# Turning x and the normalised residual by DMA, and moving the output projection, in a cross-attention and FFN kernel

## The reference, cut to what matters

```python
x = x + xattn(layernorm(x), ctx)      # 4 batches, 512 rows, 512 columns
x = x + ffn(layernorm(x))             # 1376 inner columns

def xattn(x, y):                      # 16 heads of 32
    q = ln(x @ Wq + bq)               # normalised per head
    k, v = ln(y_main @ Wk + bk), y_main @ Wv + bv        # the 496 first context rows
    k2, v2 = ln(y_dca @ Wkv_dca + ...), ...              # the 16 last ones
    return (softmax(q k) v + softmax(q k2) v2) @ Wo + bo

def ffn(x):                           # weights are lut[idx], 16 entries
    return (silu(x @ gate) * (x @ up)) @ down
```

## Time and profile before

| | |
|---|---|
| median of 3 runs | 907.59 us (905.56 to 909.68) |
| profiled execution | 908.92 us |
| its span | 907.1 us |
| PE / DVE / ACT / POOL busy | 88% / 58% / 54% / 27% |
| mean granted TensorE clock | 0.964 of full speed |

### The profile page before, as it was taken

How to read it: one execution, slowest core, us unless ns; L and a number is a source line. 1 busy time by engine, 2 the same in 40 slices (tenths; PEclk the granted TensorE clock), 3 DMA queues, 4 the chain that set the end, 5 groups by cost and what they waited for, 6 DMA issues and landing times.

```text
span 907.1 us, 15618 instructions
## 1 busy us (share of the span) xinstructions
PE 799.5 (88%) x5892; PEld 319.0 (35%) x5892; DVE 522.1 (58%) x934; ACT 487.4 (54%) x964; POOL 240.8 (27%) x284
## 2 busy tenths in 40 slices
PE   3756666699889999999899999999999999979998
PEld 1321122233345333332444333334443332234443
DVE  7759999687564888221646984216458940052220
ACT  3456567677335788554246886652558865511100
POOL 7693100000156222100472222003732210002320
PEclk9986688899999999999999999999999999999999
DMA  8349844354400000112000000101000000000001
GB/s 266 98 135 293 222 131 111 90 143 117 134 1 0 2 1 1 36 47 59 26 1 1 1 1 24 48 24 47 1 1 1 1 24 25 24 24 1 1 7 40
DMA packets 45098, 50.08 MB, mean 55 GB/s; under 512 B 5984, under 2 KB 33120, under 8 KB 45024
## 3 DMA queue, kind: packets, MB, share of 16 engines
q1 hardware_dynamic: 44688, 48.81, 18.5%
q10 hardware_dynamic: 208, 0.26, 0.1%
q0 software_dynamic: 128, 0.00, 0.0%
HBM read 40.61 MB, written 8.45 MB: 54 GB/s over the span
## 4 chain that ended last, share of the span: by engine, by line
PE 41%; issue 26%; DVE 17%; POOL 7%; ACT 7%; DMA 1%; DVEq 0%; POOLq 0%; SPq 0%; ACTq 0%
PE ps L1108 29%; DVE arena L780 5%; DVE nmax L918 4%; PE ps L1305 3%; PE ps L1288 3%; PE ps L1261 3%; ACT ps L664 3%; POOL hrstd L524 2%; ACT arena L690 2%; POOL xrstd L492 1%; POOL arena L487 1%; PE ps L1154 1%; DVE arena L919 1%; DMA arena<-in_x 1%; DVE stat L811 1%
## 5 line engine op out<-in xcount | busy, mean ns | idle before, releaser
L1108 PE MATMUL ps<-arena,wf_hi 128*128 128x512 f16 (+1 forms) x704 | 211.9, 383 | 4.3 <-DVE arena L787 1.6
L664 ACT ACTIVATE ps<-ps,nmax 128x496 f32<-128x496 f32 x256 | 165.0, 645 | 67.1 <-DVE arena L919 66.0
L690 ACT ACTIVATE arena<-ps 128x1024 f32<-128x1024 f32 x128 | 125.4, 1023 | 78.9 <-PE ps L1294 78.8
L918 DVE TENSOR_REDUCE nmax<-ps 128x2 f32<-128x992 f32 x128 | 151.9, 1187 | 22.7 <-PE ps L1261 22.7
L1108 PE MATMUL ps<-arena,wf_lo 128*128 128x512 f16 (+1 forms) x352 | 134.2, 381 | 0.0
L524 POOL TENSOR_TENSOR hrstd<-hvar,mhalf 128x16 f32<-128x16 f32 x32 | 93.8, 2932 | 134.1 <-DVE hvar L861 134.0
L1108 PE MATMUL ps<-wf_hi,arena 128*128 128x512 f16 (+1 forms) x352 | 114.1, 380 | 0.1
L1108 PEld LDWEIGHTS ps<-arena,wf_hi 128*128 128x128 f16 (+1 forms) x704 | 66.5, 100 | 93.0 <-DVE arena L787 11.1
L780 DVE TENSOR_SCALAR arena<-arena,wf_lo 128x2048 f16<-128x2048 f16 (+1 forms) x132 | 94.1, 779 | 6.3 <-DMA arena<-idx 3.7
L1154 PE MATMUL ps<-arena,wf_lo 128*32 128x512 f16 (+1 forms) x1056 | 76.5, 432 | 22.8 <-ACT wf_lo L592 21.2
L492 POOL TENSOR_TENSOR xrstd<-xvar,mhalf 128x1 f32<-128x1 f32 x32 | 18.0, 564 | 267.4 <-DVE xvar L816 267.2
(11 more groups left out here) (135 smaller groups left out, 1027.4 us busy)
## 6 DMA issues: line engine op xcount, KB each, us to landing
arena<-idx SPq DMA_DIRECT2D x124, 128.0 KB, 2.8
arena<-in_x SPq DMA_DIRECT2D x32, 256.0 KB, 2.9
wf_lo<-in_idx SPq DMA_DIRECT2D x10, 512.0 KB, 5.6
out<-arena SPq DMA_DIRECT2D x16, 256.0 KB, 2.0
idx<-wf_hi SPq DMA_DIRECT2D x10, 384.0 KB, 3.2
wf_lo<-in_idx SPq DMA_DIRECT2D x11, 256.0 KB, 6.3
arena<-in_ctxT SPq DMA_DIRECT2D x4, 512.0 KB, 5.0
arena<-in_Wq SPq DMA_DIRECT2D x4, 256.0 KB, 6.7
```

What stands on the lines that cost most here:

```text
L664: last = act.activation(sc, sc, ACT.Exp, bias=nmax[:, 0, t, h:h + 1], accum_out=den[:, 0, t, h:h + 1])
L690: act.activation(probs[n_ % 2][:, 2 * p:2 * p + 2, :], ps[:, bank:bank + 2, :], ACT.Exp).then_inc(s["probs_set"], 1)
L918: dve.tensor_reduce(nmax[:, 0, t, 2 * p:2 * p + 2], sc[:, :, DCA:S], AX_X, ALU.max, negate=True)
L1108: last = pe.matmul(dst, l, r, start=(first and i == 0), stop=(stop and i == len(todo) - 1))
```

## The change

- **x in the loop.** PE no longer transposes the tiles of the next batch's x. ACT (`stage`) copies the normalised tile to an f16 high half in its own row layout, DVE subtracts for the low half, and SP issues two transposing DMAs per tile, from the two halves to `xT[0]` and `xT[1]`. The staging buffers `x_st` lie in `xT2`. `project(0)` waits for all eight DMAs (`xt1`).
- **The normalised residual in the loop.** The same with `x2_st` (in the region of the FFN's inner result) and `xT2`; the first gate piece waits for eight transposing DMAs (`xt2`). Batch 0's x and batch 3's residual are still transposed on PE.
- **Order at the start of a pass.** PE does `project(0)`, `project(1)` and then the four Wo products; the sixteen transposes are gone, and so is a wait on `lo2` in `turn_heads`. DVE does `variance(0)`, `variance(1)`, then residual and norm per tile with `normalise(0)` and `normalise(1)` behind tiles 0 and 1, then four stages. POOL does `rstd(1)` ahead of the residual's.
- **SP's list.** The waits on `ps1` become waits on the staged halves (`staged`). In the loop two x loads are issued between the residual's transposes, and stores are split from the refills behind them so that x's transposes stand in between. In the prologue each x tile's two DMAs stand ahead of a chunk's `load_rep`.

```diff
+        x_st = [[xT2[i]...[:, t * D:(t + 1) * D] for t in range(T)] for i in range(2)]
+        x2_st = [[arena[:, a_h + (T + 2 * i) * D:...].bitcast(F16)[:, t * D:(t + 1) * D] for t in range(T)]
...
@@ sync
+            def staged(kind, t, bt, val):
+                sp.wait_ge(s[f"hi{kind}"], val(nth(bt, T, t + 1)))
+                sp.wait_ge(s[f"st{kind}"], val(nth((bt[0], bt[1] - 1) if kind == 1 else bt, T, t + 1)))
+            def turn(kind, t):
+                st, dst = (x_st, xT) if kind == 1 else (x2_st, xT2)
+                for i in range(2):
+                    sp.dma_start_transpose(dst[i][:, :, t * P:(t + 1) * P], st[i][t]).then_inc(s[f"xt{kind}"], 16)
-            next_x = {4: (0, 1), 22: (2,), 25: (3,)}
+            next_x = {4: (0, 1), 21: (2,), 24: (3,)}
+            turn_x = {21: 0, 24: 1, 27: 2, 30: 3}
             for c in range(2, NCH):
...
+                if c in turn_x:
+                    staged(1, turn_x[c], (0, 1), plain)
+                    turn(1, turn_x[c])
...
             with sp.Fori(0, B - 2) as b:
...
+                    staged(2, 2 * t + 1, (b, 0), sp.snap)
+                    load_x(t, src[t], xs[t])
+                    for t_ in range(2 * t, 2 * t + 2):
+                        turn(2, t_)
+                replace(b, 0, sp.snap, res)
+                for t in range(2):
+                    staged(1, t, (b, 2), sp.snap)
+                    load_x(t + 2, src[t + 2], xs[t])
+                    turn(1, t)
+                for t in range(2, T):
+                    staged(1, t, (b, 2), sp.snap)
+                    store(b, t - 1, sp.snap)
+                    turn(1, t)
+                    refill(b, t - 1, sp.snap, res)
+                replace(b, T - 1, sp.snap, res)
...
             for t in range(T):
+                staged(2, t, (B - 2, 0), plain)
+                turn(2, t)
@@ scalar
+            def stage(kind, t, bt):
+                act.wait_ge(s[f"xn{kind}"], nth(bt, T, t + 1))
+                src, st = (xs[t % 2], x_st) if kind == 1 else (ln2[t], x2_st)
+                act.activation(st[0][t], src, ACT.Copy).then_inc(s[f"hi{kind}"], 1)
@@ vector
+            def stage(kind, t, bt):
+                dve.wait_ge(s[f"hi{kind}"], nth(bt, T, t + 1))
+                src, st = (xs[t % 2], x_st) if kind == 1 else (ln2[t], x2_st)
+                dve.tensor_tensor(st[1][t], src, st[0][t], ALU.subtract).then_inc(s[f"st{kind}"], 1)
...
                     variance(a, 0)
-                    tail(prev)
                     variance(a, 1)
-                    normalise(a, 0, False)
-                    tail_end(prev)
+                    for t in range(T):
+                        residual(t, prev)
+                        norm(2, t, prev)
+                        if t < 2:
+                            normalise(a, t, False)
+                    for t in range(T):
+                        stage(2, t, prev)
@@ tensor
-                    pe.wait_ge(s["lo2"], nth(f, T, T))
+                        pe.wait_ge(s["xt2"], nth(f, 32 * T, 32 * T))
...
-                        pe.wait_ge(s["lo1"], nth(a, T, t + 1 if prev is None else T))
+                        pe.wait_ge(*((s["lo1"], t + 1) if prev is None else (s["xt1"], nth(a, 32 * T, 0))))
...
                 project(0)
-                if prev is not None:
-                    tail(prev)
                 project(1)
...
-                    tail_end(prev)
+                    tail(prev)
...
-                    if nxt is not None and n_ in TURN_AT:
...
-                        turn(1, TURN_AT[n_], nxt, XB, xs[TURN_AT[n_] % 2])
```

More of the change, by code:

```diff
@@ L211, in xattn_ffn @@
         ln2 = [arena[:, a_h + i * D:a_h + (i + 1) * D] for i in range(T)]
+        x_st = [[xT2[i].rearrange("p k s -> p (k s)")[:, t * D:(t + 1) * D] for t in range(T)] for i in range(2)]
+        x2_st = [[arena[:, a_h + (T + 2 * i) * D:a_h + (T + 2 * i + 2) * D].bitcast(F16)[:, t * D:(t + 1) * D] for t in range(T)]
+                 for i in range(2)]
+        assert a_h + 2 * T * D <= at[0]
         a_s = at[0]
@@ L407, in _ @@
             for t in range(T):
-                replace(B - 2, t, lambda v: v, last)
+                staged(2, t, (B - 2, 0), plain)
+                turn(2, t)
             for t in range(T):
-                store(B - 1, t, lambda v: v)
+                replace(B - 2, t, plain, last)
+            for t in range(T):
+                store(B - 1, t, plain)
             for t in range(T):
@@ L529, in core @@
                 else:
+                    rstd(1)
                     tail(prev)
@@ L532, in core @@
                     before(u)
-                    if u + 1 < NU:
+                    if u + 1 < NU and (u or prev is None):
                         rstd(u + 1)
@@ L611, in tail @@
                 for t in range(T):
-                    turn(2, t, b, LB2[t])
+                    stage(2, t, b)
             def square(a, u, first):
@@ L827, in norm @@
                 standardise(kind, t, bt, src, dst)
+            def stage(kind, t, bt):
+                staged = (bt[0], bt[1] - 1) if kind == 1 else bt
+                dve.wait_ge(s[f"hi{kind}"], nth(bt, T, t + 1))
+                src, st = (xs[t % 2], x_st) if kind == 1 else (ln2[t], x2_st)
+                dve.tensor_tensor(st[1][t], src, st[0][t], ALU.subtract).then_inc(s[f"st{kind}"], 1)
             def turn(kind, t, bt, bank):
@@ L850, in tail @@
                     norm(2, t, b)
-            def tail_end(b):
-                for t in range(T):
-                    turn(2, t, b, LB2[t])
             def variance(a, u):
@@ L1086, in _ @@
             tail((B - 1, 0))
-            tail_end((B - 1, 0))
+            for t in range(T):
+                turn(2, t, (B - 1, 0), LB2[t])
             for it in range(IT):
@@ L1111, in _, with ffn @@
             both = lambda f: [f(0), f(1)]
-            def ffn(f, piece):
+            def ffn(f, piece, last_batch=False):
                 wf = (wf_hi, wf_lo)
@@ L1136, in ffn @@
                 if a == 0 and kind == "gate" and part == 0:
-                    pe.wait_ge(s["lo2"], nth(f, T, T))
+                    if last_batch:
+                        pe.wait_ge(s["lo2"], T)
+                    else:
+                        pe.wait_ge(s["xt2"], nth(f, 32 * T, 32 * T))
                 if a and part == 0:
@@ L1171, in tail @@
                             + [(sel["o"][:, :], b16[:, :])]).then_inc(s["wo_done"], 1)
-            def tail_end(b):
-                for t in range(T):
-                    turn(2, t, b, LB2[t], ln2[t])
             def core(a, between, nxt, prev):
@@ L1227, in turn_heads @@
                         pe.wait_ge(s["tr_hi"], nth(a, NU, u - 1))
-                    elif prev is not None:
-                        pe.wait_ge(s["lo2"], nth(prev, T, u + 1))
                     for g in range(G):
@@ L1343, in _ @@
             tail((B - 1, 0))
-            tail_end((B - 1, 0))
+            for t in range(T):
+                turn(2, t, (B - 1, 0), LB2[t], ln2[t])
             for piece in PIECES:
-                ffn((B - 1, 0), piece)
+                ffn((B - 1, 0), piece, True)
 def kernel(**inputs):
```

40 lines of the change are left out of this document (17 added, 23 removed).

## The result

The changed kernel takes 935.2 us (median of 4, 934.63 to 935.95) against 907.19 beside it on the same chip: ratio 1.0309, 95% interval 1.0287 to 1.0332. The profiled execution has a span of 933.5 us against 907.1, and a mean granted clock of 0.948 against 0.964.

What follows compares the result with a forecast made beforehand. PE was taken to bound the second attention phase, a chain on other engines the start of a pass; -3.1 - 0.5 + 0.8 + 2 x 7.7 + 6.4 + 6.9 = +25.9 us on 907.6 gave 933.5, range 905 to 975.

Steps and rivals of the forecast that it cites:

- x's turns: Second attention phase: without x's sixteen PE transposes, each of two looped passes gains 1.54 us, -3.1 in all.
- The prologue: Prologue's second attention phase: removed PE transposes gain, limited by x's DMAs ahead of index loads on SP; -0.5 us.
- The premise that 2.7 us of issue per tile are free: Prologue, SP: the next index load waits for DVE's one-hot anyway, so only issue time beyond 2.7 us delays the look-up.
- DVE's chain behind the new order: Start of second pass: Wo 2.81 us later, one normalise saved; projection 4 at 456.6, against 456.57 before.
- Nothing: Start of a pass: Wo behind the projections and the removed lo2 waits were to gain nothing in the second pass.
- The wait: First gate piece: PE waits for eight transposing DMAs, losing 7.7 us in each looped pass and 6.4 in the third.
- the third chain's 0.8: Start of third pass: DVE's chain ran tighter before, so the new order makes projection 4 later, +0.8 us.
- the landing: Residual's DMAs: time from the last issue's end until the data have landed, taken as about 1.7 us.
- t, the price of an issue: SP's queue: each transposing DMA of four 128x128 blocks costs four plain issues of 0.34, 1.36 us.
- the rival above it (the blocks one after another, 1065): Residual's and prologue's DMAs: each block costs 1.36 us in turn, t = 5.44, +157 us, 1065; chance 0.05.
- The clock: Behind PE's waits for the residual's DMAs: granted clock falls to 0.50, 2.3 us in each of three passes, 6.9.

Runs made afterwards that it cites:

- e1: Against the kernel before: only x of the next batch turned by DMA, residual's transposes on PE, old order; 905.94 us, ratio 0.9988.
- e3: Against the kernel before: only the new order at the start of a pass, all transposes on PE; 917.51 us, ratio 1.0106.
- e8: Against the changed kernel: residual turned block by block, 32 DMAs of 128x128 per pass instead of 8 of 128x512; 1026.79 us, ratio 1.1328.
- e7: Against the changed kernel: a tile's two residual halves turned by one DMA of 128x1024, four per pass; 923.55 us, ratio 1.0189.
- e4: Against the changed kernel: 48 useless matmuls of 128x512 on PE ahead of the first gate piece; 929.65 us, ratio 1.0268.
- e2: Against the kernel before: only the residual turned by DMA, with the new order, x still on PE; 934.96 us, ratio 1.0319.
- e5: Against the changed kernel: Wo back behind the first projection, both halves still by DMA; 929.62 us, ratio 1.0255.
- e6: Against e5: the FFN's first gate piece moved from ahead of projection 4 to behind it; 916.35 us, ratio 1.0092.
- e9: Against e1: 13 useless matmuls in the tail, around its last group of transposes; 904.4 us, ratio 0.9976.
- e11: Against e10: nine useless matmuls per pass where PE's sixteen transposes stood; 907.41 us, ratio 0.9994.
- e10: Against e5: residual turned by two DMAs of 128x2048 per pass instead of eight, each a half of all four tiles; 909.36 us, ratio 1.0022.

## Why the prediction was right

It said 933.5 us, and 935.2 was measured. Most steps held, one held for a wrong reason, one small one failed (the prologue), and small errors cancelled: in the profiles the prologue, the waits and the clock came out 1.1, 0.6 and 0.5 us lower than forecast, and the loop's jump, which the sum didn't have, 2.3 higher. The sum of 25.9 stands against 26.4 between the profiles and 28.0 between the medians.

- **x's turns**: -3.1 forecast, -1.53 and -1.52 in the second phases. Right for the loop. In time `e1` shows a third of it, as x's turns also cost in the prologue.
- **The prologue**: -0.5 forecast, and this step failed. x's DMAs don't hide behind the look-up: in the phase where they stand, the changed kernel takes 2.6 us longer (66.85 against 64.28), and the other kernels with x by DMA 1.0 to 2.2 longer, as DVE waits for indices (11.6 us in all, 3.7 before). The premise that 2.7 us of issue per tile are free didn't hold. The issues themselves took no more, 2.50 to 3.45 us a pair; they, and SP's wait for the staged tile ahead of them, stand in front of loads that were issued earlier before. The total of -1.6 hides it and is not the change's: the changed kernel enters this phase 4.8 us earlier than the one before (164.11 against 168.91), and over all kernels that moment lies anywhere between. Why, no run shows.
- **DVE's chain behind the new order**: projection 4 due 29.8 us behind projection 0, as before. In the changed kernel DVE's normalise for it ends 32.2 us behind projection 0's start (466.17 - 433.98), of which 1.69 are projection 0's low clock: 30.5, 0.7 more than summed, of which the stages' start accounts for 0.4. Right within that, and hidden by the DMAs there. "Nothing" was too kind as a general verdict: `e3` shows 3 to 4.5 us per pass where PE's transposes must wait for the later norms.
- **The wait**: 22.6 us forecast with the third chain's 0.8 (7.7 twice, 6.4, 0.8), 22.0 measured (7.84, 7.79, 6.38). In the looped passes SP began 0.7 us later than summed and stood 0.36 between its two batches; the issues took 10.2 and not 10.9, and the landing 1.33 and not 1.7. In the third, where nothing stood between, only the two savings show, 0.8.
- **t, the price of an issue**: 1.36 forecast, 1.28 measured. The reason was wrong: it isn't four blocks at a plain issue's price, as one block costs the same 1.27. The nearest row gave the right number by luck, and the rival above it (the blocks one after another, 1065) had a price per block as well; both fell with `e8` and `e7`.
- **The clock**: 6.9 forecast, 6.4 behind the waits (1.24 three times; 0.56, 0.42, 1.69). Right in mechanism and size, and `e4` takes it away. Not foreseen: the loop's jump, +2.3, and in the variants the fall behind waits of only 2.2 us. That no gap of this stage exceeds 1.84 us and that the clock is full described the kernel before; I didn't ask what an edit does that stretches those gaps by 0.4 us.

Of the Trainium skill: VectorE: DVE Perf Modes (The three transpose paths) gives 1309 ns for one 128x128 block by DMA. `e8` has 1.27 us of issue for such a DMA, which is near it, and 2.4 from issue to landing; the page doesn't say which of the two it means. Either way it is a price of the DMA, and the 5.2 us for four blocks that I had worked out from it as an estimate stand against 1.28 in the trace. Advanced Engine Details and Errata (X-Bar Transpose (TRN2)) calls these DMAs as fast as regular ones: from issue to landing that fits (2.5 us against 2.9 and 2.8 for loads), on the issuing queue it doesn't (1.28 against 0.34), and here the queue decides.

**What stays open.** The gap at the loop's jump varies from 1.67 to 3.70 us between kernels; I don't know why. In the profiles, projection 0 behind a gap of 1.67 to 1.91 us (before, e1, e2, e3, e4) took 2.76 us, and behind 2.03 to 2.29 (after, e5, e6, e7, e9, e11) and 3.35 and 3.70 (e8, e10) 4.1 to 4.5. It need not be the code of the pass: `e9`, which differs from `e1` only in the tail, has a gap of 2.05 and projection 0 in 4.39 where `e1` has 1.71 and 2.76. Whether each execution of a kernel has the same gap isn't known, since one of each is profiled; `e4`'s two groups of times would fit one that varies, but that is argued, not shown. Of the 3.0 us that x's turns give in `e1`'s loop, the prologue's phase takes back 1.4, and the ratio shows 1.1; the difference is within its interval.

## What to carry to other kernels

Cost a transposing DMA by its issues, one after the other on the queue, and by who waits for the last of them: merge blocks into one DMA before moving the work off TensorE, and look at the loads that are queued behind it. Before taking work off a busy engine, ask what ends its waits there: here sixteen transposes filled time that VectorE's chain needed, and without them a 2 us wait brought the half clock. And work moved from one side of a wait to the other is not free on both sides: the gate's piece cost nothing ahead of projection 4 and 1.3 us behind it.

## What the runs showed of the hardware

- A transposing DMA from SBUF to SBUF holds SP's queue for 1.27 us (128x128), 1.28 (128x512; up to 1.43 in one row of eight), 1.30 (128x1024) and 1.8 to 3.1 (128x2048, all f16), each in rows of its kind; x's pairs of 128x512, between other DMAs, took 2.5 to 4.1. The medians from issue to landing are 2.4 to 3.1 us, one per kernel and with sizes mixed. A plain load of 256 KB beside it holds it for 0.34.
- The granted clock of TensorE falls to 1.2 GHz behind waits of little over 2 us in otherwise dense work: projection 2 takes 4.45 us behind a wait of 2.22 and 2.76 behind one of 0.47. It didn't in every pass: projection 2 took 2.76 behind the same 2.22 in `e5`'s first pass, and behind 2.03 in `e10`'s third. Traffic of DMAs by itself isn't what lowers it: in the latter the DMA engines are 0.73 busy at a granted clock of 1.00, and behind the changed kernel's waits 0.00 at 0.50.
- Useless matmuls in such gaps keep it at 2.4 GHz: the gate's piece takes 1.30 us in `e4` and 2.54 without them, projection 2 takes 2.76 in `e11` and 4.45 in `e10`. In the medians that is 5.5 and 2 us.
